# Expert results added up in DRAM by an accumulating scatter, four sums per token in place of six rows

## The chip, the cores and the metric
The kernel runs on 1 core of a Trainium2 chip. The metric is device time in microseconds (us) of one execution; of three runs of the kernel before the median was 1647.67 us (1644.37 to 1648.11). Everything is float32.

The engines of the core work side by side and wait for each other only at semaphores: TensorE (PE, its weight loads are PEld), VectorE (DVE), ScalarE (ACT), GpSimd (POOL) and SyncE (SP). SP issues most of the DMAs from its queue; POOL issues the indirect ones, whose target rows are given by a column of indices. All DMAs run on the same 16 DMA engines.

## The reference, cut to what matters
A block of 4096 tokens of 256 numbers goes through a mixture of experts (FFN), a local and a global attention, and the same FFN again:

```python
x = x + 0.5 * ffn(layernorm(x))
x = x + attention(layernorm(x))
x = x + 0.5 * ffn(layernorm(x))

def ffn(x):                              # 4096 tokens, 256 wide, 32 experts, 6 per token
    scores = sigmoid(x @ gate.T);  sfc = scores + bias
    # 4 of the 8 groups of experts by their best sfc, then the 6 best experts of these
    _, topk_idx = top_k(where(group_kept, sfc, 0), 6)
    tw = take(scores, topk_idx);  tw = tw / tw.sum() * 2.5
    routed = sum over the 6 chosen experts e of tw_e * ((silu(x @ g_e.T) * (x @ u_e.T)) @ dn_e.T)
    shared = (silu(x @ sg.T) * (x @ su.T)) @ sd.T
    return routed + shared
```

## The kernel before, in words
`x` stays in SBUF (`xres`, 32 tiles of 128 tokens). Each FFN has three stages, and each engine runs its own written-out program through them. The order on an engine is that of the code; there is no scheduler.

**Routing** (`*_route`; in the second FFN it is woven into the attention, `*_pass_b`) goes by 16 pairs of tiles. DVE normalizes a pair, PE transposes it and makes the logits, DVE finds the six experts and each token's place among the rows of each expert (`v_route_groups`, `v_route_six`, `v_route_ranks`, `v_route_weights`, `v_route_slots`). A row of 320 floats is built for each token: 256 of the normed token, 32 weights (`COL_W`) and 32 destinations (`COL_DEST`), the latter from a running count over the chosen experts (`nth`) and the token's number times six (`tok6`). POOL scatters each row six times, once per expert, into `dispatch_rows` in DRAM (line 522: 12 indirect DMAs per pair). SP stores the transposed token tiles to `normed_transposed` (line 409), and in the first FFN it also loads the experts' weights between these stores (`load_experts`, lines 398 to 403), a piece per pair.

**Experts** (`*_experts`) works through 224 blocks of 128 dispatched rows. SP loads a block into one of four buffers `blk` (line 437). PE transposes it (line 638), multiplies by gate and up (`wgu`), transposes the gated result (line 667), and multiplies by `wdn`. DVE takes the block's weight column and destination column out of the row (`pick`, line 1325, twice), multiplies (line 1337), adds to the destination an offset that pushes rows beyond the block's last one out of bounds (line 1345), and copies the result from PSUM into one of four buffers `yb` (line 1347). POOL scatters the 128 rows of `yb` into `answers` (line 535), where each token has six rows of its own; rows out of bounds are not written. DVE may overwrite a `yb` buffer once the scatter from it, four blocks earlier, has landed (`s.scat`).

**Combining** (`*_combine`) goes tile by tile. SP loads the tile's transposed tokens (line 449) and its six answer rows per token in two DMAs, of four rows and of two (line 457). DVE adds them in pairs: 0+2 and 1+3 (line 1405), 4+5 (line 1408). POOL adds the three results to `xres` (line 549). PE computes the shared expert (16 and 4 weight loads by the trace's count), and DVE adds it (line 1389). The answers have two buffers (`ans`), so a tile's load is issued when the sum of two tiles earlier is done (`s.red`).

## Time and profile before

| | |
|---|---|
| time, median of 3 runs | 1647.67 us |
| the profiled execution, first to last instruction | 1952.5 us |
| PE busy | 1406.0 us (72%) |
| DVE busy | 1173.1 us (60%) |
| POOL busy | 985.2 us (50%) |
| ACT busy | 643.7 us (33%) |
| moved by DMA | 283.75 MB, mean 145 GB/s |
| read from DRAM / written | 152.10 MB / 139.46 MB |

The profiled execution has only its span, 1952.5 us; what lies around it is not shown, and it is already 304.8 us longer than the median of the runs. A duration of one instruction is read from it as it stands; the length of a whole stage may be longer than in a run without the profiler.

By stages of the span: routing of the first FFN 0 to 345 us, its table of blocks to 367, experts to 779, combining to 886, the global attention to 940, local attention with the second routing to 1400, table to 1430, experts to 1840, combining to the end.

### The profile page before, as it was taken

The page shows a single profiled execution, that of the slowest core. Times are in us where ns is not written, and L with a number is a line of the kernel's source. Part 1 is how long each engine was busy: PE and PEld are TensorE (multiplying, and loading weights), DVE is VectorE, ACT ScalarE, POOL GpSimd, SP SyncE. Part 2 cuts the span into 40 slices and gives each one's busy share as a digit, 9 for nine tenths or more (in the row PEclk, how much of TensorE's full clock was granted, in tenths as well). Part 3 has the DMA queues.
Part 4 walks back from the last instruction along what each step waited for, and adds up shares of the span by engine and source line. Part 5 has one row for each costly group of instructions (what it writes and reads, how often), then busy time and mean ns, then how long its engine had stood idle before and what let it go on. Part 6 is the DMA issues. An engine that isn't in the chain of part 4 may idle for free.

```text
span 1952.5 us, 48288 instructions
## 1 busy us (share of the span) xinstructions
PE 1406.0 (72%) x8734; PEld 1125.2 (58%) x8735; DVE 1173.1 (60%) x5408; ACT 643.7 (33%) x2344; POOL 985.2 (50%) x1050
## 2 busy tenths in 40 slices
PE   2211121499999999886877676776369999999996
PEld 2111111377777778873655464554257777777795
DVE  5444444466666666794565564645656666666586
ACT  1000000244444444110643343434134444454310
POOL 3555555355555555780043424334545555555587
PEclk9999999999999999997987777878579999999998
DMA  8444444345545553880021212112244554555498
GB/s 280 161 165 154 150 153 148 101 152 163 164 152 158 160 163 105 297 294 0 7 76 67 84 59 80 71 66 92 95 133 152 163 165 148 159 160 160 133 318 305
DMA packets 165350, 283.75 MB, mean 145 GB/s; under 512 B 30118, under 2 KB 117691, under 8 KB 165312
## 3 DMA queue, kind: packets, MB, share of 16 engines
q1 hardware_dynamic: 121216, 165.78, 28.1%
q0 software_dynamic: 39936, 113.33, 15.9%
q10 hardware_dynamic: 4160, 4.19, 0.6%
q8 instruction: 16, 0.26, 0.1%
q14 instruction: 22, 0.18, 0.0%
HBM read 152.10 MB, written 139.46 MB: 149 GB/s over the span
## 4 chain that ended last, share of the span: by engine, by line
PE 39%; DVE 20%; issue 16%; SPq 6%; another core or an unknown queue 6%; DMA 5%; POOL 4%; ACT 2%; DVEq 1%; POOLq 0%; ACTq 0%
PE ps L566 32%; PE ps L638 4%; POOL xres L549 3%; SPq L432 3%; DMA ans<-answers 2%; SPq L437 2%; PE ps L667 2%; DVE prob L1519 1%; DMA blk<-dispatch_rows 1%; DVE newt L1119 1%; DVE newt L1118 1%; DVE yb L1405 1%; DVE rstd L1120 1%; DVE ohs L1223 1%
## 5 line engine op out<-in xcount | busy, mean ns | idle before, releaser
L535 POOL DMA_INDIRECT answers<-yb,didx x448 | 441.2, 985 | 399.1 <-issue 302.9
L522 POOL DMA_INDIRECT dispatch_rows<-blk,idx x384 | 376.2, 980 | 520.5 <-DVE idx L1225 409.2
L566 PE MATMUL ps<-wgu,xbt 128*128 x1792 | 471.4, 386 | 3.4 <-ACT xbt L967 1.2
L566 PEld LDWEIGHTS ps<-wgu,xbt 128*128 128x128 f32 x1792 | 308.6, 192 | 35.7 <-issue 10.7
L566 PE MATMUL ps<-wdn,hbt 128*128 x896 | 278.6, 393 | 25.5 <-DVE yb L1347 16.1
L1337 DVE SCALAR_TENSOR_TENSOR hb<-ps,wcol,sg 128x128 f32<-128x128 f32 x448 | 157.2, 351 | 229.1 <-ACT sg L973 153.7
L1325 DVE SCALAR_TENSOR_TENSOR picked<-iota_e,etab,blk 128x32 f32<-128x32 f32 x896 | 190.3, 250 | 47.2 <-DMA blk<-dispatch_rows 11.5
L973 ACT ACTIVATE sg<-ps 128x128 f32<-128x128 f32 x448 | 124.7, 278 | 250.5 <-PE ps L566 128.8
L566 PEld LDWEIGHTS ps<-wdn,hbt 128*128 128x128 f32 x896 | 156.4, 190 | 80.7 <-issue 63.1
L967 ACT COPY xbt<-ps 128x256 f32<-128x256 f32 x448 | 167.5, 374 | 106.3 <-PE ps L638 100.2
L1347 DVE COPY yb<-ps 128x256 f32<-128x256 f32 x448 | 187.3, 418 | 13.2 <-remote 6.7
L638 PE MATMUL ps<-ident,blk 128*128 128x128 f32 x896 | 176.3, 279 | 20.4 <-DMA blk<-dispatch_rows 19.2
L977 ACT COPY hbt<-ps 128x128 f32<-128x128 f32 x448 | 119.2, 266 | 146.5 <-PE ps L667 109.1
L573 PE MATMUL ps<-ident,yb 128*128 128x128 f32 x128 | 35.5, 371 | 169.0 <-issue 90.4
L638 PEld LDWEIGHTS ps<-ident,blk 128*128 128x128 f32 x896 | 110.5, 143 | 66.9 <-DMA blk<-dispatch_rows 35.5
L566 PEld LDWEIGHTS ps<-blk,wsgu 128*128 128x128 f32 x1024 | 126.9, 197 | 9.5 <-DMA blk<-normed_transposed 6.4
L566 PE MATMUL ps<-blk,wsgu 128*128 128x128 f32 x1024 | 129.0, 281 | 3.1 <-DMA blk<-normed_transposed 3.1
L667 PE MATMUL ps<-ident,hb 128*128 128x128 f32 x448 | 122.6, 274 | 0.0
L549 POOL TENSOR_TENSOR xres<-xres,yb 128x256 f32 (+1 forms) x128 | 108.2, 845 | 27.6 <-DVE yb L1405 16.0
L573 PEld LDWEIGHTS ps<-ident,yb 128*128 128x128 f32 x128 | 21.7, 212 | 172.8 <-issue 101.8
L934 ACT COPY xnt<-ps 128x256 f32<-128x256 f32 x64 | 23.9, 373 | 239.6 <-PE ps L573 161.2
L1507 DVE TENSOR_REDUCE smax<-ps 128x8 f32<-128x512 f32 x32 | 22.1, 690 | 132.8 <-remote 127.4
(180 smaller groups left out, 2139.6 us busy)
## 6 DMA issues: line engine op xcount, KB each, us to landing
blk<-dispatch_rows SPq DMA_DIRECT2D x448, 160.0 KB
ans<-answers SPq DMA_DIRECT2D x64, 512.0 KB, 4.4
ans<-answers SPq DMA_DIRECT2D x64, 256.0 KB, 4.2
normed_transposed<-xnt SPq DMA_DIRECT2D x64, 128.0 KB
wgu<-in_gate_up SPq DMA_DIRECT2D x32, 256.0 KB
blk<-normed_transposed SPq DMA_DIRECT2D x64, 128.0 KB, 3.5
answers<-yb,didx POOLq DMA_INDIRECT x448
dispatch_rows<-blk,idx POOLq DMA_INDIRECT x384
```

The costliest lines, as they stand in the source:

```text
L522: pool.indirect_dma_start(out=rows_dram, out_offset=bass.IndirectOffsetOnAxis(ap=idx[:, q, k:k + 1], axis=0), in_=rows[:, q, :], in_offset ...
L535: pool.indirect_dma_start(out=answers_dram, out_offset=bass.IndirectOffsetOnAxis(ap=didx[:, q:q + 1], axis=0), in_=yb[:, q, :], in_offset= ...
L549: pool.tensor_tensor(xtile(i), xtile(i), sums, ALU.add).then_inc(s.part, 1)
L566: return nc.tensor.matmul(out_, lhs, rhs, start=start, stop=stop)
L638: m = pe.transpose(ps[:, TX + q % 2, c * P:(c + 1) * P], blk[:, q, c * P:(c + 1) * P], ident[:])
L667: pe.transpose(ps[:, HT + 1 - j, 0:P], hb[:, 1 - j, :], ident[:]).then_inc(s.ht, 1)
L967: act.copy(xbt[:, j, :], ps[:, TX + j, 0:D]).then_inc(s.xt, 1)
L973: act.activation(sg[:, j, :], ps[:, GU + j, 0:I], ACT.Silu).then_inc(s.sg, 1)
L977: act.copy(hbt[:, 1 - j, :], ps[:, HT + 1 - j, 0:P]).then_inc(s.hts, 1)
L1325: v.scalar_tensor_tensor(out=picked[:, k, :], in0=iota_e[:], scalar=etab[:, bass.ds(n, 1)], in1=blk[:, q, col:col + E], op0=ALU.is_equal, ...
L1337: v.scalar_tensor_tensor(out=hb[:, j, :], in0=ps[:, GU + j, I:2 * I], scalar=wcol[:, q:q + 1], in1=sg[:, j, :], op0=ALU.mult, op1=ALU.mult ...
L1347: v.tensor_copy(yb[:, k, :], ps[:, DN + j, 0:D]).then_inc(s.y, 1)
```

## The change: what it does
1. The scatter of an expert's result adds to the row in DRAM (`compute_op=ALU.add`) in place of writing a row of its own. There are four tensors of sums (`answer_sums0` to `3`, 4096+128 rows of 1 KB each); block `n` adds into sum `n % 4`, whose buffer `yb[n % 4]` is also reused only when that scatter has landed, so no two scatters into one sum are under way together. Rows beyond a block's end are no longer left out: they go to row 4096 + partition, which nobody reads.
2. The sums are zeroed by SP during each routing (`zero_sums`): per pair of tiles four DMAs of 256 KB, and with the first pair four more of 128 KB for the last rows. POOL waits for all of them before the first scatter of an FFN.
3. A dispatched row has one destination (the token's number) in place of 32: 289 floats in place of 320. The running count `nth` goes from the routing, and in the experts stage the second `pick` and the addition of the offset become one instruction on 128x1 numbers.
4. Combining loads four rows per token, in four DMAs of 128 KB, adds them with one DVE instruction, and POOL adds two results to `xres` in place of three.

```diff
-ROW = D + 2 * E
+ROW = D + E + 1
-NOWHERE = 2 * T * TOPK
+NOWHERE = 2 * T
+NACC = 4
-        answers_dram = nc.dram_tensor("answers", [T * TOPK, D], F32).ap()
+        sums_dram = [nc.dram_tensor(f"answer_sums{k}", [T + P, D], F32).ap() for k in range(NACC)]
+        def zero_sums(sp, p):
+            for k in range(NACC):
+                sp.dma_start(sums_dram[k][bass.ds(p * (2 * P), 2 * P)].rearrange("(a p) d -> p a d", p=P),
+                             padt[:, 0:D].unsqueeze(1).to_broadcast([P, 2, D])).then_inc(zeroed, 16)
+                if isinstance(p, int):
+                    sp.dma_start(sums_dram[k][T:T + P], padt[:, 0:D]).then_inc(zeroed, 16)
             def load_answers(i, j):
-                for k, (a, b) in enumerate(PARTS):
-                    positive(sp, s.red, i * 2 - 3 + k)
-                    part = slice(a * D, b * D)
-                    sp.dma_start(ans[:, j, part], ans_v[bass.ds(i, 1)][:, :, part].rearrange("a p d -> (a p) d")
-                                 ).then_inc(s.ans[k][j], 16)
+                positive(sp, s.red, i - 1)
+                for k in range(NACC):
+                    sp.dma_start(ans[:, j, k * D:(k + 1) * D], sums_dram[k][bass.ds(i * P, P)]
+                                 ).then_inc(s.ans[j], 16)
         def pool_experts(pool, s):
-            with pool.Fori(0, NB // 4) as g:
-                for q in range(4):
-                    pool.wait_ge(s.y, g * 4 + (q + 1))
+            pool.wait_ge(zeroed, 16 * ZEROS * (s.n + 1))
+            pool.sem_inc(s.take, 1)
+            with pool.Fori(0, NB // 8) as g:
+                for r in range(8):
+                    q = r % 4
+                    pool.wait_ge(s.y, g * 8 + (r + 1))
                     pool.sem_inc(s.take, 1)
                     pool.indirect_dma_start(
-                        out=answers_dram, out_offset=bass.IndirectOffsetOnAxis(ap=didx[:, q:q + 1], axis=0),
-                        in_=yb[:, q, :], in_offset=None, bounds_check=T * TOPK - 1,
-                        oob_is_err=False).then_inc(s.scat[q], 16)
+                        out=sums_dram[q], out_offset=bass.IndirectOffsetOnAxis(ap=didx[:, r:r + 1], axis=0),
+                        in_=yb[:, q, :], in_offset=None, compute_op=ALU.add).then_inc(s.scat[q], 16)
         def v_route_weights
-            for t in range(2):
-                st.did(v.tensor_tensor_scan(nth[:, t, :], ones[:, 0:E], sel[:, t, :], 0.0, ALU.mult, ALU.add))
-            for t in range(2):
-                st.did(v.tensor_scalar(rows[:, 2 * k + t, COL_DEST:ROW], nth[:, t, :],
-                                       tok6[:, bass.ds(p * 2 + t, 1)], None, ALU.add))
+            st.did(v.tensor_copy(rows[:, two, COL_DEST], token_of[:, bass.ds(p * 2, 2)]))
         def v_experts, pick
-                for k, (col, out_) in enumerate(((COL_W, wcol), (COL_DEST, dcol))):
-                    v.scalar_tensor_tensor(
-                        out=picked[:, k, :], in0=iota_e[:], scalar=etab[:, bass.ds(n, 1)],
-                        in1=blk[:, q, col:col + E], op0=ALU.is_equal, op1=ALU.mult,
-                        accum_out=out_[:, q:q + 1]).then_inc(s.pick, 1)
+                v.scalar_tensor_tensor(
+                    out=picked[:], in0=iota_e[:], scalar=etab[:, bass.ds(n, 1)],
+                    in1=blk[:, q, COL_W:COL_W + E], op0=ALU.is_equal, op1=ALU.mult,
+                    accum_out=wcol[:, q:q + 1]).then_inc(s.pick, 1)
+                v.scalar_tensor_tensor(
+                    out=didx[:, r:r + 1], in0=skip[:, bass.ds(n, 1)], scalar=blk[:, q, COL_DEST:COL_DEST + 1],
+                    in1=dump[:], op0=ALU.add, op1=ALU.min).then_inc(s.pick, 1)
         def v_experts, step
-                    st.did(v.tensor_tensor(didx[:, k:k + 1], dcol[:, k:k + 1], skip[:, bass.ds(n - 2, 1)], ALU.add))
                     v.wait_ge(s.d, n - 1)
                     v.tensor_copy(yb[:, k, :], ps[:, DN + j, 0:D]).then_inc(s.y, 1)
-                    st.sync()
         def v_combine, body
                 v.tensor_tensor(two_sums[j], a[:, 0:2, :], a[:, 2:4, :], ALU.add).then_inc(s.red, 1)
-                v.wait_ge(s.ans[1][j], 16 + visits(i, j, 2, 16))
-                positive(v, s.part, i * 3 - 3)
-                v.tensor_tensor(third_sum[j], a[:, 4, :], a[:, 5, :], ALU.add).then_inc(s.red, 1)
         block.sync
                 load_experts(sp, p)
+                zero_sums(sp, p)
-            sp_route(sp, R[1])
+            sp.wait_ge(C[0].red, NT)
+            sp_route(sp, R[1], lambda p: zero_sums(sp, p))
```

DVE in the middle of the experts stage (`hb` is the gated result, `yb` the buffer that is scattered; `ans` in these rows is the memory that holds the table of offsets), before:

```order
L1337 SCALAR_TENSOR_TENSOR hb<-ps,wcol,sg 128x128 [waits ex_pick_0,ex_ht_0,ex_sg_0]
L1345 TENSOR_TENSOR didx<-dcol,ans 128x1
L1347 COPY yb<-ps 128x256 [waits ex_d_0]
L1325 SCALAR_TENSOR_TENSOR picked,wcol<-iota_e,etab,blk 128x32 [waits ex_pick_0,ex_h_0,ex_ld1_0,vector_step]
L1325 SCALAR_TENSOR_TENSOR picked,dcol<-iota_e,etab,blk 128x32
```

The same block of DVE's program after:

```order
L1342 SCALAR_TENSOR_TENSOR hb<-ps,wcol,sg 128x128 [waits ex_pick_0,ex_ht_0,ex_sg_0]
L1351 COPY yb<-ps 128x256 [waits ex_d_0]
L1326 SCALAR_TENSOR_TENSOR picked,wcol<-iota_e,etab,blk 128x32 [waits ex_h_0,ex_pick_0,ex_ld1_0]
L1331 SCALAR_TENSOR_TENSOR didx<-ans,blk,dump 128x1
```

The instruction on `didx` moved from ahead of the copy to behind the pick, and one of the two picks on 128x32 is gone.

SP's queue in the loop of combining, for one tile (`cb_gu`: the shared gate and up of an earlier tile is done; `cb_red`: the sum of two tiles earlier), before:

```order
L449 ISA [waits cb_gu_0]
L449 DMA blk<-normed_transposed 128x256
L49 ISA
L457 ISA [waits cb_red_0]
L457 DMA ans<-answers 128x1024
L49 REGISTER_ALU
L457 ISA [waits cb_red_0]
L457 DMA ans<-answers 128x512
```

and after:

```order
L458 ISA [waits cb_gu_0]
L458 DMA blk<-normed_transposed 128x256
L465 ISA [waits cb_red_0]
L465 DMA ans<-answer_sums 128x256 x4
```

The two loads of a tile's answers, each behind its own wait, became four loads behind one wait.

SP's queue in the loop of the first routing, for one pair, after (before, it ended with the loads of `wgu`):

```order
L420 DMA normed_transposed<-xnt 128x256
L400 ISA
L400 DMA dispatch_rows<-padt 128x289
L400 ISA
L400 DMA dispatch_rows<-padt 128x289
L401 ISA
L401 DMA wdn<-in_down 128x512
L405 REGISTER_ALU
L405 DMA wgu<-in_gate_up 128x512
L405 ISA
L405 DMA wgu<-in_gate_up 128x512
L409 ISA
L409 DMA answer_sums<-padt 128x2x256 x4
```

Four DMAs of 256 KB now stand between a pair's stores and the next pair's.

## Rows read from the trace of the kernel before

**Rows 1.** Windows by stage: busy us of each engine, granted clock, DMA share, GB/s.
```profile
0.00:345.00 345.00, 75.80 (x288) 59.36 (x289) 164.76 (x746) 26.21 (x66) 183.30 (x211) 1.00 0.50 172
367.00:779.00 412.00, 390.31 (x2053) 317.65 (x2054) 266.77 (x1570) 191.47 (x675) 219.81 (x224) 1.00 0.50 152
779.00:886.00 107.00, 87.92 (x605) 80.26 (x603) 91.75 (x208) 11.53 (x30) 82.56 (x97) 0.93 0.80 270
940.00:1400.00 460.00, 322.77 (x2825) 238.04 (x2823) 263.98 (x1026) 194.04 (x826) 169.73 (x173) 0.78 0.19 71
```

**Rows 2.** Windows, the same columns: ten us inside one pair of the second routing.
```profile
1175.50:1185.50 10.00, 3.56 (x16) 1.36 (x20) 0.31 (x2) 1.01 (x1) 6.17 (x7) 0.61 0.31 115
```

**Rows 3.** Timeline of PEld in the experts stage: start, us, engine, line, what.
```profile
601.19 0.73 PEld L566 LDWEIGHTS ps<-wgu,xbt 128*128 128x128 f32 x4
...
602.82 0.73 PEld L566 LDWEIGHTS ps<-wgu,xbt 128*128 128x128 f32 x4
```

**Rows 4.** POOL's scatters: one of a run in routing, and all of line 535.
```profile
206.00 0.97 POOL L522 DMA_INDIRECT dispatch_rows<-blk,idx  x1 [0.30 <-issue]
...
L535 POOL DMA_INDIRECT answers<-yb,didx x448: 982/985/1004, 379.4 to 1843.2; - x150
```

**Rows 5.** The page's DMA queues: packets, MB, share of 16 engines.
```profile
q1 hardware_dynamic: 121216, 165.78, 28.1%
q0 software_dynamic: 39936, 113.33, 15.9%
```

**Rows 6.** Timeline at the end of the first experts stage.
```profile
778.64 0.98 POOL L535 DMA_INDIRECT answers<-yb,didx  x1 [2.59 <-issue]
...
781.37 1.75 SPq L457 DMA_DIRECT2D ans<-answers  x4
```

**Rows 7.** Two DVE groups of the experts stages by line: min/median/max ns, waits.
```profile
L1345 DVE TENSOR_TENSOR didx<-dcol,ans x448: 142/150/202, 377.6 to 1838.3; 128x1 int32<-128x1 f32 x150
...
L1325 DVE SCALAR_TENSOR_TENSOR picked<-iota_e,etab,blk x896: 241/250/305, 370.3 to 1834.1; 128x32 f32<-128x32 f32 x180
...
  DVE hb L1337: 22.0, 28
```

**Rows 8.** Groups of the window 800 to 870 us, in the first combining.
```profile
L549 POOL TENSOR_TENSOR xres<-xres,yb 128x256 f32 x47 | 38.3, 816 | 4.4 <-POOL xres L549 4.4
L1405 DVE TENSOR_TENSOR yb<-ans 128x512 f32<-128x512 f32 x24 | 22.0, 917 | 0.0
...
L1408 DVE TENSOR_TENSOR red<-ans 128x256 f32<-128x256 f32 x12 | 11.4, 948 | 0.0
```

**Rows 9.** Timeline of one tile of the first combining.
```profile
831.03 1.97 PEld L566 LDWEIGHTS ps<-blk,wsgu 128*128 128x128 f32 x16
...
833.09 0.73 PEld L566 LDWEIGHTS ps<-wsd,hsh 128*128 128x128 f32 x4
```

**Rows 10.** The page's DMA issues: KB each, median us from issue to landing.
```profile
ans<-answers SPq DMA_DIRECT2D x64, 256.0 KB, 4.2
...
blk<-normed_transposed SPq DMA_DIRECT2D x64, 128.0 KB, 3.5
```

**Rows 11.** Timeline of DVE in one pair of the first routing.
```profile
228.66 0.21 DVE L1202 TENSOR_TENSOR cw<-sc,sel 128x64 f32<-128x64 f32 x1
228.80 0.39 DVE L1205 TENSOR_TENSOR_SCAN nth<-ones,sel 128x32 f32<-128x32 f32 x2
...
229.39 0.22 DVE L1210 TENSOR_REDUCE csum<-cw 128x2 f32<-128x64 f32 x1 [0.20 <-issue]
229.53 0.39 DVE L1212 TENSOR_SCALAR blk<-nth,tok 128x32 f32<-128x32 f32 x2
```

**Rows 12.** Timeline of DVE: first work behind a pair's last routing step (second routing).
```profile
1167.43 0.68 DVE L1507 TENSOR_REDUCE smax<-ps 128x8 f32<-128x512 f32 x1
```

**Rows 13.** The start: the window 0 to 30 us, and ACT's second pair.
```profile
0.00:30.00 30.00, 7.84 (x30) 6.01 (x31) 16.60 (x80) 3.93 (x9) 6.42 (x29) 1.00 0.90 286
...
32.63 0.37 ACT L934 COPY xnt<-ps 128x256 f32<-128x256 f32 x1 [10.68 <-DMA normed_transposed<-xnt]
```

More of the change, by code:

```diff
@@ L266, in build @@
         padded = sem("padded")
+        zeroed = sem("zeroed")
         consts = sem("consts")
@@ L317, in __init__ @@
                 s = lambda name: sem(f"{name}_{n}")
-                self.ans = [[s(f"cb_ans{part}_{j}") for j in range(2)] for part in range(2)]
+                self.ans = [s(f"cb_ans{j}") for j in range(2)]
                 self.xs = [s(f"cb_xs{q}") for q in range(4)]
@@ L1344, in step @@
                              16 * ((n - 2) // 4) if isinstance(n, int) else n * 4 - (8 + 4 * k))
-                    st.did(v.tensor_tensor(didx[:, k:k + 1], dcol[:, k:k + 1], skip[:, bass.ds(n - 2, 1)], ALU.add))
                     v.wait_ge(s.d, n - 1)
                     v.tensor_copy(yb[:, k, :], ps[:, DN + j, 0:D]).then_inc(s.y, 1)
-                    st.sync()
                 if m is None or n + 2 < NB:
-                    pick(n + 2, (q + 2) % 4)
+                    pick(n + 2, (r + 2) % 8)
             pick(0, 0)
             pick(1, 1)
-            for n in range(4):
-                step(n, n % 4, m=0)
-            one = 1
-            with v.Fori(1, NB // 4 - 1) as g:
-                for q in range(4):
-                    st.rebase(g * (4 * one) + (start + q - 2))
-                    step(g * 4 + q, q)
-            st.rebase(start + NB - 4 - 2)
-            for n in range(NB - 4, NB + 2):
-                step(n, n % 4, m=0)
+            for n in range(8):
+                step(n, n, m=0)
+            with v.Fori(1, NB // 8 - 1) as g:
+                for r in range(8):
+                    step(g * 8 + r, r)
+            for n in range(NB - 8, NB + 2):
+                step(n, n % 8, m=0)
         def v_combine(v, st, s, last):
```

43 lines of the change are left out of this document (20 added, 23 removed).

## The prediction, made before the changed kernel was run
> **What bounds the kernel now.** I read the windows by stage first, since the page's shares average over stages with different limits. The two experts stages last 412 us each and PE is busy for 390 of them [rows 1]; in a stretch without a disturbance a block of 128 rows follows the last after 1.63 us (601.19 to 602.82, and the two after it the same), in which the weight loads have no gap worth naming [rows 3]. So PE sets the pace there. Over the whole stage a block takes 412/224 = 1.84 us. Combining takes 107 us for 32 tiles; DVE is busy for 92, PE 88, POOL 83: three engines near their limit, none alone. In the routings nothing is: 345 us with DVE 165 and POOL 183 busy [rows 1].
>
> Then I asked why the profiled span (1952.5 us) is 304.8 us longer than the median of the runs. Within one pair of the second routing there are ten microseconds in which PE, DVE and ACT all nearly stop, while POOL goes on issuing scatters (DVE 0.31 us busy of 10) [rows 2]. If it returned in each of the 16 pairs it would make 160 us; the first routing has the like. I take these stalls for an effect of the recording and the timed kernel as shorter mainly in the routings. That is an inference. It matters twice: a gain that is read in a stall is worth nothing, and in a timed run the first routing is near POOL's pace: 12 scatters at 0.97 + 0.30 = 1.27 us make 15.3 us per pair [rows 4], 244 us for 16 pairs. My sum is in us of unstalled rows, so that it can be set against either: span 1952.5 or median 1647.7.
>
> **Part 1, the scatter into the sums.** The instruction is there 448 times as before, and its duration is 0.985 us now; the scatter without a bounds check, in routing, takes 0.97 [rows 4]. The trace has no accumulating DMA, so three costs are open.
> (a) POOL's own time. Hidden as long as duration plus 0.30 stays under PE's 1.63, that is up to 1.33 us. Lower bound 0.97, upper bound: twice the row, 1.97, which makes 2.27 us a block, +0.64 x 448 = +287 us. I take 0.98, the nearest row: the indices and rows that POOL handles are as many as before.
> (b) Time of the DMA engines. POOL's queue used 15.9% of the span for 832 scatters: 0.159 x 1952.5 / 832 = 0.37 us of all 16 engines per scatter. SP's queue used 0.281 x 1952.5 = 549 us for 121216 packets, 0.072 us per packet on one engine, so a block's load of 128 rows is 128/16 x 0.072 = 0.58 us [rows 5]. Together 0.95, under 1.63. An accumulating scatter reads its target as well. Bounds: 0.37 (the addition is free) and 4 x 0.37 = 1.5 (every row moved four times); I take twice, 0.75: it reads rows from two places in place of one, and of the two ends the plain scatter is the row at hand. 0.58 + 0.75 = 1.33 is still hidden. The point from which it isn't is 1.63 - 0.58 = 1.05 us, 2.8 times the plain scatter; at the upper bound a block takes 2.08, +0.45 x 448 = +200 us. That rows beyond a block's end are now written (448 x 128 = 57344 in place of 49152) is +17% and within this.
> (c) Landing. From the end of the last scatter's issue, 778.64 + 0.98 = 779.62, to SP's first load behind it, 781.37, are 1.75 us [rows 6]. A `yb` buffer is free for four blocks, 6.5 us, of which copy, wait and issue take some 2; landing may take 4.5 before DVE waits. I take 3.5 us. Hidden but for the end of each stage, where combining waits for the last: 2 x 1.75 = +3.5 us.
>
> The Trainium skill bears on (b): "Collectives: The Full Stack", section "The bandwidth ceiling", says that a reducing transfer is not slowed by the addition but by its two source reads, and moves data at about half a copy's rate. No row here shows it. By it the engines' time doubles, as I took it, and rival A needs more than that; the sum by the plain row alone would be the same, since both are hidden.
>
> **Part 2, zeros.** Per routing 4 x 4224 x 1 KB = 17.3 MB more. Combining moves 270 GB/s at a DMA share of 0.80, so 337 GB/s at full share, and the zeros are 51 us of all engines. The first routing has 0.50 x 345 = 172 us of DMA work [rows 1], 223 with them, against some 245 to 345 us of stage: room, but not much in a timed run. The second has 0.19 x 460 = 87, 138 with them: hidden. At the very start there is no room: the first 30 us run at a share of 0.90, and ACT already waits 10.68 us for the stores of the first pair, which stand in the same queue [rows 13]. The zeros of the first pair (1.57 MB, 5 us at 337 GB/s) now stand ahead of the second pair's stores, and 3 us more ahead of each of the next. Later pairs follow POOL's pace, so this is paid about once: +5 us. Bounds 0 (POOL's pace absorbs it) and +14 (5 + 3 x 3). The wait on `zeroed` costs nothing: all zeros are issued with the last pair's stores, and the table of blocks (some 22 us) lies between these and the first scatter.
>
> **Part 3, one destination per row.** In routing DVE loses two scans and two additions per pair. The scans: the sum `csum` starts at 229.39 behind `cw`, which ends at 228.87; without the scans between them it starts some 0.15 later than that, 0.37 earlier than now. The additions take 0.39 where one copy of 128x2 takes about 0.15 [rows 11]: together 0.6 us per pair. In the second routing this is on the path: DVE goes from the last routing step of a pair into the next tile's maximum without an idle time (its row names none) [rows 12], for which ACT and PE wait. 16 x 0.6 = 9.7; I take -8. In the first routing POOL's 15.3 us per pair bound a timed run, and I take 0 (it would be -9.6 if DVE set the pace). In the experts stage DVE loses 0.15 and one of two picks with its accumulator read, 0.25 + 0.08, and gains one instruction on 128x1, about 0.15: 0.3 us per block off an engine that is busy 267 of 412. PE bounds, so nearly nothing; but the gated product waited 22.0 us for picks, 28 times [rows 7], and so I take -3, between 0 and -22. Rows of 289 floats in place of 320 are 10% fewer bytes in a queue that isn't full: 0.
>
> The Trainium skill speaks against gaining from the narrower row: "DMA: Bandwidth & Descriptors", section "How a descriptor splits into AXI transactions", says that a read that doesn't start at a multiple of 256 B is fetched from the boundary below. 320 floats are 1280 B, five such pieces; 289 are 1156 B and nearly never start on one, so about as much is fetched. No row here shows it. Without the rule a block's load would take 0.52 us of the engines in place of 0.58 and a scatter could take 1.11 before it binds; with it the point stays at 1.05.
>
> **Part 4, combining.** 24 tiles in 70 us are 2.92 us a tile [rows 8]. Per tile DVE loses the instruction of line 1408 (0.95 us) and POOL one of three additions (at least 0.82). PE remains with 1.97 + 0.73 = 2.70 [rows 9]. But the loads now bind: a buffer is filled again only behind the sum of two tiles earlier. SP issues four loads, 0.44 us apart (1.75 for four [rows 6]), the last lands 3.5 us later (the row for 128 KB [rows 10]), and the sum takes 0.68 to 0.92: 1.32 + 3.5 + 0.8 = 5.6 us for two tiles, 2.80 a tile. So PE and the loads are within 0.1 of each other. Before, one load of 4.2 us and one sum made 5.1. I take 2.80: 64 x 0.12 = -8 us. Bounds: PE's 2.70, -14 us; and landing no faster than the 256 KB load, 4.2, with the sum at 0.92: 3.2 a tile, +19 us. The first sum of each combining waits for two more issues per tile, 3 x 0.44 = 1.3 us: +3.
>
> **Sum.** +3.5 (last scatters) + 5 (start) - 8 (second routing) - 3 (experts) - 8 + 3 (combining) = -7.5 us: span 1945, median 1647.7 - 7.5 = 1640.
>
> **Rivals.**
> A, the scatter becomes the bound (slower). Mechanism: a block's accumulating scatter takes more than 1.33 us of POOL or 1.05 us of the DMA engines, and PE waits through `yb` for `s.scat`. For it speaks that nothing in the trace shows the price, and that 448 blocks multiply it: 0.1 us of excess is 45 us. Against it the slack in (a) to (c). With POOL's 0.985 half as long again, 1.48 + 0.30 = 1.78 a block, +0.15 x 448 = +67, the time is 1707; three times the DMA time, 0.58 + 1.12 = 1.70, makes +31 and 1671.
> B, DVE's relief counts fully (faster). The waits for picks go (-22 more or less), the first routing is DVE's after all (-9.6), combining reaches PE's 2.70: 1640 - 19 - 9.6 - 6 = 1605, with the half of it 1622.
> C, the gains are eaten: SP's five DMAs and their landing keep combining at 2.92 a tile and the crowded start costs 14: 1640 + 8 + 9 = 1657, with one of the two 1648.
> That the change doesn't do what it says would need sums still read as six rows; SP's rows show four, so I give it nothing.
>
> **How the numbers follow.** Forecast 0.50 (its own range 1630 to 1650), A 0.24, B 0.12, C 0.14. A measurement of this kernel tells 0.3% (5 us) from no change; faster is below 1642.7. The forecast's half gives 0.30 faster, 0.14 same, 0.06 slower; B 0.12 faster; C 0.07 same and 0.07 slower; A 0.24 slower. Faster 0.42, same 0.21, slower 0.37. The range takes in C, half of B and A up to half as long again on POOL: 1615 to 1712; what lies beyond are the upper bounds of (a) and (b), 1840 and more, and B in full.
>
> **What would show it.** The line of the scatter still at 0.97 to 1.0 us and experts stages of 412 us or a little less: Part 1 right. Scatter above 1.33 us, or DVE's copy to `yb` waiting for DMAs: A. The DMA share in the experts windows from 0.50 to about 0.7 shows twice the engine time. Tiles of combining 2.8 us apart with DVE waiting for loads: Part 4. ACT's second wait for the stores grown from 10.68 by some 5 us: Part 2. `csum` 0.15 us behind `cw`, and the second routing shorter by 8 us: Part 3. The prediction is wrong if the experts stages differ by more than 10 us, or if the zeros slow the routings all along; and the profiled stalls may themselves grow with the DMA packets, which would lengthen the span and not the time.

## The result: 5.3% slower, and the profile after

| kernel | median of the runs, us | lowest to highest |
|---|---|---|
| before | 1646.02 | 1642.23 to 1648.11 |
| after | 1731.97 | 1731.80 to 1734.19 |

The ratio is 1.0533 (95% interval 1.0517 to 1.055): +86 us. 1640 had been forecast, with a range of 1615 to 1712, and 1731.97 lies above the range too.

The profiled execution of after has a span of 1732.4 us, no longer than its runs. That of before had 304.8 us more than its median, so stages can't be compared with it. The first experiment below records the unchanged kernel again, with a span of 1649.1 us; all comparisons by stage are made with that recording. It is of the slowest of that kernel's eight runs, 3.6 us over their median, so a difference of a stage is sure to some 3 us only. The stages follow from the starts of POOL's scatters and of the first instruction of the second FFN's routing; the second routing ends here where its last scatter starts:

| stage | before, us | after, us | difference | forecast |
|---|---|---|---|---|
| start to the first scatter of an expert | 288.0 | 293.9 | +5.9 | +5 |
| experts 1, first to last scatter | 363.5 | 415.9 | **+52.4** | -1.5 |
| combining 1 and global attention | 146.2 | 137.6 | -8.7 | -0.75 |
| local attention and second routing | 362.1 | 351.4 | -10.6 | -8 |
| table of blocks, to the first scatter | 15.1 | 13.8 | -1.3 | 0 |
| experts 2 | 363.9 | 414.2 | **+50.3** | -1.5 |
| combining 2 to the end | 110.3 | 105.6 | -4.7 | -0.75 |

(The forecasts of Part 3's -3 and of Part 4 with the last scatters, -8 + 3 + 3.5, are halved over the two stages of a kind.) The differences sum to +83.3, the difference of the spans. Two stages lose 103 us and the rest gains 19.

The windows by stage (those of experts and of the second routing reach to the end of the last scatter, 1 us further than the table; window, its length, then busy us of PE, PEld, DVE, ACT and POOL with their instructions, granted clock, DMA share, GB/s), first of the unchanged kernel's second recording, which answers to [rows 1]:

```profile
0.00:288.00 288.00, 87.51 (x336) 69.04 (x338) 175.91 (x810) 31.28 (x79) 192.67 (x219) 1.00 0.63 216
288.00:652.50 364.50, 363.62 (x2024) 317.37 (x2024) 262.16 (x1543) 186.13 (x663) 220.21 (x224) 1.00 0.56 168
...
797.70:1160.80 363.10, 276.60 (x2988) 219.83 (x2988) 286.26 (x1103) 202.73 (x864) 190.82 (x192) 0.89 0.27 98
```

and of after:

```profile
0.00:293.90 293.90, 86.76 (x332) 68.43 (x334) 168.16 (x753) 30.81 (x78) 191.71 (x220) 0.97 0.78 258
293.90:711.40 417.50, 401.72 (x2032) 302.47 (x2031) 242.47 (x1103) 186.37 (x664) 349.51 (x224) 1.00 0.92 148
...
847.40:1199.80 352.40, 267.45 (x2988) 212.40 (x2988) 277.74 (x1055) 203.02 (x864) 191.66 (x192) 0.92 0.41 142
```

In the experts stage before, PE is busy for all of it (363.62 of 364.50). From the first to the last of the 224 scatters are 363.5 us and 223 steps: a block takes 1.63 us. After, POOL's 224 scatters cost 349.51 us in place of 220.21, the DMA share is 0.92 in place of 0.56, and the GB/s fall. PE's busy time has grown with the stage, to 401.72 of 417.50: the same matmuls, stretched by waits that the profile counts into them. Read alone, that row still looks like a kernel bound by PE; the weight loads, which shrank from 317.37 to 302.47 while the stage grew, say that it isn't.

Rows of POOL's timeline in the middle of that stage (start, duration, what, idle time before it), which answer to [rows 4]:

```profile
402.13 1.56 POOL L546 DMA_INDIRECT answer_sums<-yb,didx  x1 [0.30 <-issue]
404.00 1.56 POOL L546 DMA_INDIRECT answer_sums<-yb,didx  x1 [0.31 <-issue]
405.87 1.56 POOL L546 DMA_INDIRECT answer_sums<-yb,didx  x1 [0.30 <-DVE yb L1351]
```

One scatter starts every 1.86 us: 1.56 of its own and the 0.30 that stood between scatters of a run in routing before. So there is no slack left on POOL, and 415.9/223 = 1.865 is the stage's own pace. The page's queues, to be held against [rows 5], and its groups of the scatter and of the copy to `yb`:

```profile
q0 software_dynamic: 82944, 115.59, 39.9%
q1 hardware_dynamic: 175616, 176.01, 34.5%
...
L546 POOL DMA_INDIRECT answer_sums<-yb,didx x448 | 697.3, 1556 | 162.8 <-issue 123.1
...
L1351 DVE COPY yb<-ps 128x256 f32<-128x256 f32 x448 | 189.7, 423 | 305.9 <-DMA answer_sums<-yb,didx 298.3
```

Two suspects stand here side by side. POOL issues the scatter for 1556 ns in place of 985. And DVE waits 298.3 us for scatters to land, while q0's share has grown to 39.9%. In the window 400 to 500 us the queues' shares are these:

```profile
q0 software_dynamic: 7696, 7.01, 64.5%
q1 hardware_dynamic: 7739, 7.95, 28.8%
issues: line engine op xcount, KB each, median us to landing
blk<-dispatch_rows SPq DMA_DIRECT2D x53, 144.5 KB
answer_sums<-yb,didx POOLq DMA_INDIRECT x54
```

64.5/54 = 1.19 us of all 16 engines per scatter and 28.8/53 = 0.54 per load, together 1.73 us a block: over PE's 1.63 as well, and under POOL's 1.86. Which of the two sets the pace is what most experiments ask. One row of this trace bears on it already, the first scatter of the stage:

```profile
293.88 1.61 POOL L546 DMA_INDIRECT answer_sums<-yb,didx  x1 [14.05 <-DVE yb L1351]
```

In the 12.8 us before it (281 to 293.8) not one packet of POOL's queue moves, so no earlier scatter can hold it up, and it takes 1.61 us all the same; the first of the second stage takes 1.60. The length is the instruction's own and not a wait behind a full queue.

### The profile page after: what moved, and what is told of

Same layout as the page of the kernel before. It is cut to its first block, busy times and chain, and to the rows that moved or that the text cites. A ratio compares the mean times of both kernels' runs of the same rounds, so it can differ in the third digit from the quotient of the medians.

```text
span 1732.4 us, 46430 instructions
## 1 busy us (share of the span) xinstructions
PE 1359.6 (78%) x8734; PEld 1061.8 (61%) x8735; DVE 1058.4 (61%) x4352; ACT 643.6 (37%) x2344; POOL 1174.1 (68%) x987
## 3 DMA queue, kind: packets, MB, share of 16 engines
q0 software_dynamic: 82944, 115.59, 39.9%
## 4 chain that ended last, share of the span: by engine, by line
issue 23%; DMA 22%; POOL 20%; PE 13%; DVE 12%; SPq 5%; ACT 1%; POOLq 1%; DVEq 1%; ACTq 0%
DMA answer_sums<-yb,didx 17%; PE ps L576 11%; POOL answer_sums L546 10%; POOL dispatch_rows L531 10%; DMA ans<-answer_sums 4%; SPq L465 3%; DVE yb L1351 2%; DVE prob L1517 1%; ACT ans L1054 1%; PE ps L881 1%; DVE yb L1406 1%; DMA dispatch_rows<-blk,idx 1%; DVE smax L1505 1%; DVE stats L1143 1%; PE ps L648 1%
## 5 line engine op out<-in xcount | busy, mean ns | idle before, releaser
L546 POOL DMA_INDIRECT answer_sums<-yb,didx x448 | 697.3, 1556 | 162.8 <-issue 123.1
L1351 DVE COPY yb<-ps 128x256 f32<-128x256 f32 x448 | 189.7, 423 | 305.9 <-DMA answer_sums<-yb,didx 298.3
L576 PEld LDWEIGHTS ps<-wgu,xbt 128*128 128x128 f32 x1792 | 306.6, 191 | 38.2 <-issue 12.8
L576 PE MATMUL ps<-wdn,hbt 128*128 x896 | 290.2, 406 | 15.0 <-DVE yb L1351 12.3
L576 PEld LDWEIGHTS ps<-wdn,hbt 128*128 128x128 f32 x896 | 145.0, 189 | 102.8 <-issue 94.8
L648 PE MATMUL ps<-ident,blk 128*128 128x128 f32 x896 | 172.8, 275 | 33.7 <-DMA blk<-dispatch_rows 33.7
L559 POOL TENSOR_TENSOR xres<-xres,yb 128x256 f32 (+1 forms) x128 | 93.5, 731 | 98.1 <-DVE yb L1406 86.5
L677 PE MATMUL ps<-ident,hb 128*128 128x128 f32 x448 | 127.7, 285 | 12.8 <-DVE hb L1342 12.7
L1326 DVE SCALAR_TENSOR_TENSOR picked<-iota_e,etab,blk 128x32 f32<-128x32 f32 x448 | 112.5, 251 | 31.4 <-DMA blk<-dispatch_rows 31.4
L677 PEld LDWEIGHTS ps<-ident,hb 128*128 128x128 f32 x448 | 62.8, 140 | 65.9 <-DVE hb L1342 56.7
L1406 DVE TENSOR_TENSOR yb<-ans 128x512 f32<-128x512 f32 x64 | 46.8, 731 | 82.2 <-DMA ans<-answer_sums 74.0
L1331 DVE SCALAR_TENSOR_TENSOR didx<-ans,blk,dump 128x1 int32<-128x1 f32 x448 | 96.5, 215 | 0.0
```

The lines of the kernel that those rows point to most:

```text
L546: pool.indirect_dma_start(out=sums_dram[q], out_offset=bass.IndirectOffsetOnAxis(ap=didx[:, r:r + 1], axis=0), in_=yb[:, q, :], in_offset= ...
L576: return nc.tensor.matmul(out_, lhs, rhs, start=start, stop=stop)
L648: m = pe.transpose(ps[:, TX + q % 2, c * P:(c + 1) * P], blk[:, q, c * P:(c + 1) * P], ident[:])
L677: pe.transpose(ps[:, HT + 1 - j, 0:P], hb[:, 1 - j, :], ident[:]).then_inc(s.ht, 1)
L1326: v.scalar_tensor_tensor(out=picked[:], in0=iota_e[:], scalar=etab[:, bass.ds(n, 1)], in1=blk[:, q, COL_W:COL_W + E], op0=ALU.is_equal, op ...
L1331: v.scalar_tensor_tensor(out=didx[:, r:r + 1], in0=skip[:, bass.ds(n, 1)], scalar=blk[:, q, COL_DEST:COL_DEST + 1], in1=dump[:], op0=ALU.a ...
```

## The experiments

Ratios are against the kernel before, run beside them on the same chip.

### The unchanged kernel, recorded again


> The kernel before once more, for a second profile of it. In its first profile the span was 1952.5 us against timed runs of 1646, with stretches in which every engine nearly stood. If these stretches belong to that one recording, this profile's span lies within 5 us of the timed runs, an experts stage lasts 224 x 1.63 to 1.70 = 365 to 380 us and a pair of the second routing about 21 us. If they belong to the kernel under any recording, the span is again above 1900.

Measured: 1647.47 us, ratio 0.9998 (0.9983 to 1.0013), span 1649.1. The experts stages last 363.5 and 363.9 us, just under the 365 to 380 expected. The 304.8 us of stalls in the first recording are not the kernel's. No recording of after or of the kernels below has any, though POOL's queue moves twice the packets in after (82944 against 39936). What set them off in that one stays open.

### The scatter writes in place of adding
```diff
-    in_=yb[:, q, :], in_offset=None, compute_op=ALU.add).then_inc(s.scat[q], 16)
+    in_=yb[:, q, :], in_offset=None).then_inc(s.scat[q], 16)
```
All else is as in after; the sums then hold only each row's last write.

> The changed kernel with a plain write in the scatter in place of the addition (the sums are then wrong: the last block's row stays). Theory issue: the addition makes POOL's instruction 1.56 us in place of 0.97, and 1.56 + 0.30 = 1.86 per block is over PE's 1.63; theory landing: it makes the DMA work of a scatter about 1.2 us of all engines and its landing 4.9, and DVE waits for the buffer. Both expect POOL's instruction at 0.97, experts stages of 365 to 380 us, and a time of 1732 - 2 x (416 - 372) = 1644, less if the other parts gain what I forecast (1636 to 1646). Rival rest: the zeros, the dump rows and the four loads cost the 86 us; then the time stays above 1700.

Measured: **1630.31 us, ratio 0.9899 (0.9882 to 0.9915)**. First the window of its first experts stage, then POOL's timeline and POOL's queue in the window 400 to 500 us (62 scatters):

```profile
293.70:658.70 365.00, 364.12 (x2028) 318.72 (x2027) 218.14 (x1103) 186.80 (x664) 217.50 (x224) 1.00 0.55 169
```
```profile
399.39 0.97 POOL L546 DMA_INDIRECT answer_sums<-yb,didx  x1 [0.57 <-issue]
401.09 0.97 POOL L546 DMA_INDIRECT answer_sums<-yb,didx  x1 [0.73 <-issue]
```
```profile
q0 software_dynamic: 2928, 8.00, 20.2%
```

Scatter 0.97, idle time of 0.57 and 0.73 before these two, PE bound again; the time is 6 us under the range expected (1636 to 1646), since the stages are shorter than the 372 us it was reckoned with. One keyword costs 1731.97 - 1630.31 = 102 us, all of it in the experts stages (364.0 and 364.0 us). Against the kernel before, run beside this one (1647.41), zeros, routing, combining and the row format together gain 17 us. Excess by POOL's cadence: (1.86 - 1.63) x 448 = 103.

### Eight buffers and eight sums
```diff
-        sums_dram = [... for k in range(NACC)]
+        sums_dram = [... for k in range(8)]
...
-                    k = (q + 2) % 4
+                    k = (r + 6) % 8
...
-                    v.tensor_copy(yb[:, k, :], ps[:, DN + j, 0:D]).then_inc(s.y, 1)
+                    v.tensor_copy(result(k), ps[:, DN + j, 0:D]).then_inc(s.y, 1)
```
`result(k)` is `yb` for four buffers and unused memory of the stage for the others; eight sums are zeroed and scattered into, combining still reads four of them.

> The changed kernel with eight result buffers and eight sums in the experts stage, so that a buffer is free for eight blocks and two scatters into one sum still never overlap; twice the zeros are written, and combining still reads only four of the eight sums (half of the results are left out). Theory issue: DVE's waits for landed scatters (298 us now) go, yet a block still takes 1.86 us and the experts stages stay at 416; the time is 1732 plus what 17 MB more zeros per routing cost (0 to 30). Theory landing by latency: the experts stages shrink to 365 to 380 us and the time by 80. If it is the DMA engines' work, not the latency, the stages stay at about 224 x 1.74 = 390 or more.

Measured: 1740.08 us, ratio 1.0567 (1.0545 to 1.059); scatters 1.56 us, 1.86 apart. DVE's waits in the window 400 to 500 us (engine, line, waited for: us, times, longest; `ans` names the memory of the four further buffers):

```profile
DVE yb L1354 <- DMA answer_sums<-yb,didx: 19.0, 24, 1.6
DVE ans L1354 <- DMA answer_sums<-ans,didx: 17.9, 21, 1.6
```

I had expected these waits to go. They stayed, 36.9 us against 35.8 in after, and twice the room moved nothing. So the 298.3 us are a symptom: behind a pace maker slower than PE the ring of buffers fills up, and the producer then waits for its oldest buffer, with eight as with four. The timelines of DVE's copies and POOL's scatters, matched in order, show where a result stands: from the end of its copy to the start of its scatter are 0.8 us with the plain write, 2.7 in after and 10.0 here (medians of the first stage). The results wait for POOL. Landing is not the bound. Of the 5.4 us by which its span (1737.8) exceeds after's, 4.0 lie ahead of the first scatter, where twice the zeros are written.

### Sums of half the width
```diff
-            in_=yb[:, q, :], in_offset=None, compute_op=ALU.add).then_inc(s.scat[q], 16)
+            in_=yb[:, q, 0:D // 2], in_offset=None, compute_op=ALU.add).then_inc(s.scat[q], 16)
```
The four sums have 128 columns; the second half of a result isn't added, and combining reads the first half twice.

> The changed kernel with sums of 128 numbers per row: the scatter adds only the first half of each result, and combining reads that half twice (half of the results are left out). The DMA work of a scatter falls from 1.2 to 0.6 to 0.9 us of all engines and it lands sooner; the number of rows and indices that POOL handles stays. Theory issue: POOL's instruction stays at 1.56 and the experts stages at 416. Theory landing or DMA work: the stages shrink towards 365 to 380, and POOL shows idle time between its scatters.

Measured: 1737.34 us, ratio 1.0552 (1.0535 to 1.057), first experts stage 416.1 us. Queue shares in the window 400 to 500 us, and POOL's timeline:

```profile
q0 software_dynamic: 7774, 3.54, 33.8%
q1 hardware_dynamic: 7774, 7.99, 31.7%
```
```profile
398.05 1.56 POOL L547 DMA_INDIRECT answer_sums<-yb,didx  x1 [0.30 <-issue]
399.92 1.56 POOL L547 DMA_INDIRECT answer_sums<-yb,didx  x1 [0.30 <-issue]
```

Half the bytes take half the engines' time (33.8/54 = 0.63 us per scatter in place of 1.19), the total falls to 1.21 us a block, well under PE's 1.63, and not a microsecond comes back. They also land sooner: DVE's waiting copies start 3.5 us behind the start of the scatter that frees their buffer, in after 4.4 (medians). **The DMA engines are not the bound, nor is landing, and the 1.56 us are not back-pressure of bytes.** The number of packets is unchanged, though, so this run alone doesn't exclude a price per packet. Why the time is 5 us over after's isn't explained; combining, which reads each half row twice, may be a part of it.

### One more instruction on POOL per scatter, and its control
```diff
                         in_=yb[:, q, :], in_offset=None, compute_op=ALU.add).then_inc(s.scat[q], 16)
+                    pool.wait_ge(s.fill, g * 8 + (r + 1))
+                    pool.sem_inc(ppassed, 1)
+                    pool.memset(idle[:], 0.0).then_inc(s.fill, 1)
```
(`fill` is a new semaphore, raised once ahead of the loop, so that a memset waits for the one before and not for the scatter; `idle` is 128x1.)

> The changed kernel with one more small POOL instruction behind each of the 448 scatters (a memset of 128x1, 0.1 to 0.13 us, with 0.05 to 0.2 us around it). Theory issue (POOL's 1.56 + 0.30 us per block are the bound): every block is longer by what the filler takes, 0.15 to 0.3 us, so 67 to 135 us on 1732. Rival (the landing of the scatters or the DMA engines' work is the bound, 1.74 of 1.86 us by their shares): POOL's filler fills a wait, and the time moves by less than 20 us.

The same three lines in the kernel before (with `g * 4 + (q + 1)`):

> The same filler in the kernel before, as the control. There POOL needs 1.28 us per block of PE's 1.62: with 0.15 to 0.3 more it is at 1.43 to 1.58, still below, and theory issue expects no change (within 5 us of 1647). If the filler costs the same here as in the changed kernel, it slows something else than POOL's queue, and the reading of the other run falls.

Measured: with the filler after takes 1740.69 us (ratio 1.0566, 1.0546 to 1.0585), only 8.7 more; before takes 1646.46 (1.0000, 0.9987 to 1.0012). POOL's timelines, of after with the filler and then of before with it:

```profile
400.32 0.71 POOL L554 MEMSET idle<- 128x1 f32 x1
401.23 1.57 POOL L549 DMA_INDIRECT answer_sums<-yb,didx  x1 [0.19 <-POOL idle L554]
402.21 0.70 POOL L554 MEMSET idle<- 128x1 f32 x1
403.10 1.57 POOL L549 DMA_INDIRECT answer_sums<-yb,didx  x1 [0.19 <-POOL idle L554]
```
```profile
399.19 0.13 POOL L544 MEMSET idle<- 128x1 f32 x1
399.75 0.98 POOL L538 DMA_INDIRECT answers<-yb,didx  x1 [0.43 <-POOL idle L544]
```

The control is as expected. The test is a miss: by its number alone (8.7 us, under the 20 of the expectation) it is what the rival of landing or DMA work had forecast. The rows show why it can't decide. I had taken the filler to stand behind the scatter with its full time. Its row starts 0.98 us after the scatter's start, as in the control, and lasts 0.70 us in place of 0.13; it ends 0.11 us behind the scatter, and the next scatter starts 0.30 us behind the last one, as without a filler. So the filler fits into the 0.30 us that stand between two scatters anyway, and doesn't price POOL. Whether the memset worked beside the scatter or only stood there until the scatter's end, the rows don't say.

### Half the rows
```diff
-   out=sums_dram[q], out_offset=bass.IndirectOffsetOnAxis(ap=didx[:, r:r + 1], axis=0),
-   in_=yb[:, q, :], in_offset=None, compute_op=ALU.add).then_inc(s.scat[q], 16)
+   out=sums_dram[q], out_offset=bass.IndirectOffsetOnAxis(ap=didx[0:P // 2, r:r + 1], axis=0),
+   in_=yb[0:P // 2, q, :], in_offset=None, compute_op=ALU.add).then_inc(s.scat[q], 16)
```
Rows 64 to 127 of every block are not added.

> The changed kernel whose scatter adds only the first 64 rows of each block (the other 64 results are left out). It asks what sets POOL's 1.56 us. If it goes with the rows, the instruction falls to about half plus a fixed part, 0.8 to 1.1 us, PE is the bound again, and the time is 1630 as with the plain write. If it is a fixed cost of the addition, the instruction stays near 1.56 and the time near 1732.

Measured: 1666.23 us, ratio 1.0113 (1.0094 to 1.0132). POOL's timeline:

```profile
400.75 1.40 POOL L546 DMA_INDIRECT answer_sums<-yb,didx  x1 [0.30 <-issue]
402.46 1.40 POOL L546 DMA_INDIRECT answer_sums<-yb,didx  x1 [0.30 <-issue]
```

The queues in the window 400 to 500 us (60 scatters):

```profile
q0 software_dynamic: 4720, 3.87, 37.9%
q1 hardware_dynamic: 8423, 8.65, 32.7%
```

Neither expectation was met: 64 rows fewer take off 0.16 us, 2.4 ns a row, and by a straight line through the two some 1.25 us would remain with no row at all (an estimate). The cadence of 1.71 us predicts (1.71 - 1.63) x 448 = +36 us over the plain write; measured are +35.9. POOL's 1.86 and 1.71 thus each give the loss, where the DMA work was 1.73 and is (37.9 + 32.7)/60 = 1.18, under PE's pace. The number of packets doesn't price the instruction either: 63 fewer per scatter (4720/60 = 79 in place of 142) take off 0.16 us, so the 95 that separate an adding scatter from a plain one (47) would account for 0.24 of the 0.58 us.

### The addition in every other block
```diff
-                        in_=yb[:, q, :], in_offset=None, compute_op=ALU.add).then_inc(s.scat[q], 16)
+                        in_=yb[:, q, :], in_offset=None,
+                        **({} if q % 2 else dict(compute_op=ALU.add))).then_inc(s.scat[q], 16)
```
Sums 1 and 3 are written, not added to.

> The changed kernel with the addition in every other block and a plain write in the rest (the sums are then wrong). POOL's mean per block is (1.86 + 1.27) / 2 = 1.57 us, just below PE's 1.62. Theory issue expects a time of 1630 to 1640: the loss is a threshold, not a price per addition. If each addition costs the engines its own share, half of the 102 us stays and the time is about 1681.

Measured: **1625.98 us, ratio 0.9864 (0.9848 to 0.988)**, experts stage 362.8 us.

```profile
398.99 1.58 POOL L546 DMA_INDIRECT answer_sums<-yb,didx  x1 [0.30 <-issue]
400.87 0.98 POOL L546 DMA_INDIRECT answer_sums<-yb,didx  x1 [0.30 <-issue]
402.34 1.57 POOL L546 DMA_INDIRECT answer_sums<-yb,didx  x1 [0.50 <-issue]
```

Two blocks cost POOL 1.88 + 1.28 = 3.16 us, 1.58 each, under 1.63, and idle time is back (0.50). So 224 additions in two stages cost nothing, where 448 cost 102 us: a threshold, not a price per addition. The time is 4 us under the range expected (from 1630) and under the plain write's; why isn't explained.

### The first pair's zeros behind the routing
```diff
-                zero_sums(sp, p)
+                if not isinstance(p, int):
+                    zero_sums(sp, p)
             sp_route(sp, R[0], more)
+            zero_sums(sp, 0)
```


> The changed kernel with the zeros of the first pair (1.57 MB, eight DMAs) written by SP behind the whole first routing in place of ahead of the second pair's stores. If the 5.9 us by which the first scatter of the experts now starts later come from these zeros in the crowded start, 3 to 6 us come back and the time is 1726 to 1729. If they come from the zeros of all pairs, the first scatter stays at 294 us and the time at 1732.

Measured: 1731.42 us, ratio 1.051 (1.0495 to 1.0524), against after's 1.0533 (1.0517 to 1.055) no difference that can be told, where 1726 to 1729 had been expected. ACT's wait for the second pair's stores in after and in this kernel, answering to the row of ACT in [rows 13] (there 10.68; it belongs to the third pair, not to the second as is said there):

```profile
40.84 0.37 ACT L944 COPY xnt<-ps 128x256 f32<-128x256 f32 x1 [17.90 <-DMA normed_transposed<-xnt]
```
```profile
34.81 0.37 ACT L944 COPY xnt<-ps 128x256 f32<-128x256 f32 x1 [12.48 <-DMA normed_transposed<-xnt]
```

The first scatter starts at 288.8 in place of 293.9: the 5 us at the start are these zeros, through the stores that stand behind them. In after, SP issues the eight DMAs of zeros from 28.18 to 35.34 us, and only then the second pair's stores. But the gain was lost again further on: the second routing took 354.6 us in place of 351.4, and the two combining stages 1.5 us more. For the same 2988 matmuls PE was busy 272.5 us at a mean granted clock of 0.91, after's 267.45 at 0.92. Why the clock differed is open, and so is whether the late zeros had a part in it.

### Before, with one scan and one addition per pair
```diff
-            for t in range(2):
-                st.did(v.tensor_tensor_scan(nth[:, t, :], ones[:, 0:E], sel[:, t, :], 0.0, ALU.mult, ALU.add))
+            st.did(v.tensor_tensor_scan(nth[:].rearrange("p t e -> p (t e)"), ones[:, 0:2 * E],
+                                        sel[:, 0:2, :].rearrange("p t e -> p (t e)"), 0.0, ALU.mult, ALU.add))
...
-            for t in range(2):
-                st.did(v.tensor_scalar(rows[:, 2 * k + t, COL_DEST:ROW], nth[:, t, :],
-                                       tok6[:, bass.ds(p * 2 + t, 1)], None, ALU.add))
+            st.did(v.tensor_tensor(rows[:, two, COL_DEST:ROW], nth[:],
+                                   tok6[:, bass.ds(p * 2, 2)].unsqueeze(2).to_broadcast([P, 2, E]), ALU.add))
```
The count runs on through the second tile, and `tok6` starts six lower per token there.

> The kernel before, results unchanged, with the running count of a pair in one scan over 64 numbers in place of two over 32 (each token has exactly six chosen experts, so the second tile's count starts at six, which the table of token numbers takes off), and one addition in place of two. DVE saves about 0.3 us per pair. The change gained 10.6 us in the second routing by dropping all of this (0.6 us per pair); if DVE's order is what bounds a pair there, half of it comes with this: 3 to 6 us, a time of 1641 to 1644. If the gain came from the lighter traffic of the narrower rows or from the lost wait, nothing moves.

Measured: **1643.62 us against 1645.64, ratio 0.9983 (0.9974 to 0.9993)**. The window of the second routing:

```profile
794.30:1152.20 357.90, 273.35 (x2988) 218.04 (x2988) 282.49 (x1071) 202.96 (x864) 190.45 (x192) 0.90 0.27 99
```

DVE's busy time falls by 3.8 us against 286.26, the stage by 4.2 to 357.8. A part of these 4.2 us may be chance: the recording is of this kernel's fastest run, the one that it is compared with of the slowest of its own, and in the recording of the filler in the kernel before, whose routing is unchanged, the stage took 360.8. The medians differ by 2.0 us, with 3 to 6 expected. It is the fastest kernel here that computes everything, by less than 0.2%.

## Why the prediction was wrong, point by point

**The step that failed: Part 1 (a).** "I take 0.98, the nearest row: the indices and rows that POOL handles are as many as before." The point from which it binds (1.33 us) was right, the bounds (0.97 to 1.97) held the truth, 1.56, and PE's pace was 1.63, as taken. The step that failed is the term "duration of the scatter": 0.98 us taken, 1.56 measured, so that 0.23 us a block were not hidden. It was chosen by counting POOL's inputs, and these did not change. What the instruction turns out did: q0's packets are 7696/54 = 142 per scatter in the window 400 to 500 us, where the plain write shows 2928/62 = 47 there. But by the run with half the rows that number accounts for 0.24 of the 0.58 us at most; where POOL spends the rest of them stays open. The nearest row was the row of another operation. With 1.56 in the sum the forecast had been -7.5 + 0.23 x 448 = +96 us, 1743. That is rival A, at the size of 1.48 us given as its example (1707); it was given 0.24, and with the point from which it binds, 1.33, in the lower half of the bounds of an unknown price, the chance should have been nearer to a half. The range ended at 1712 because it let POOL's row grow by half; it grew by 58%.

The Trainium skill has the reading that was missing. "Perfetto Trace Analysis", section "DMA Instruction — SWDGE (GPSIMD)", says that the profiled end of a DMA issued by GpSimd is the end of its descriptor generation, not of the data's movement. The runs agree: half the bytes leave the row at 1.56 us, fewer rows shorten it, and the data land at 4.89 us (below), well behind its end. Of the stage's first scatter, whose row ends 1.61 us after its start, no packet moves for 2.9 us. So the row's 1.56 us are work on POOL ahead of the transfer, and POOL pays for the addition. The page gives no price for it, and that the added time is spent on descriptors is not shown here.

**Part 1 (b), DMA engines: direction right, size low.** Taken 0.75 us, measured 1.19; with the load of 0.54 (taken 0.58) 1.73 a block, over PE's 1.63, and a DMA share of 0.92 in the stage where about 0.7 had been named as the sign. It stayed hidden only behind POOL. If POOL's price went, by this sum the DMA engines would bind next and leave (1.73 - 1.63) x 448 = some 45 us; that is an estimate and wasn't tried. The Trainium skill, "Collectives: The Full Stack" (section "The bandwidth ceiling") would have it at half a copy's rate, thus twice 0.33 (plain write: 20.2/62); here it is 3.6 times. The measurement decides; the page took its rule from large collectives, and for this scatter of rows of 1 KB it falls short.

**Part 1 (c), landing: hidden as forecast, size roughly right.** The chain of waits has it from the scatter's start:

```profile
400.27 4.89 DMA answer_sums<-yb,didx
```

Less the 1.56 us of issue that is 3.3 us, where 3.5 were taken; by DVE's waiting copies it lies between 3.7 and 5.3 us from the scatter's start, 4.4 in the median. At the end of the first stage, from the last scatter's start at 709.82 to SP's first load at 713.64, are 3.8 us, as at the end of the second; in the unchanged kernel's second recording they are 3.1 and 2.2. That is +2.3 for both, forecast +3.5.

**Part 2, zeros: right.** +5.9 us at the start against +5, by the mechanism named; the wait on `zeroed` cost nothing, and the second routing took the zeros at a DMA share of 0.41 without a loss that shows (352.5 us with twice the zeros, 351.4 with these).

**Part 3: the routing right, the experts stage wrong by little.** DVE's timeline in one pair of the second routing after, to be read against [rows 11]:

```profile
1000.36 0.22 DVE L1212 TENSOR_TENSOR cw<-sc,sel 128x64 f32<-128x64 f32 x1
1000.78 0.22 DVE L1216 TENSOR_REDUCE csum<-cw 128x2 f32<-128x64 f32 x1 [0.20 <-DVE cw L1212]
1000.91 0.16 DVE L1217 COPY blk<-token_of 128x2 f32 x1
```

`csum` starts 0.20 us behind `cw` (0.15 forecast), and the copy takes 0.16. DVE's busy time in that stage falls by 286.26 - 277.74 = 8.5 us, the stage by 10.6 (forecast 8). The last experiment, with about half the relief, got 4.2 by its recording and 2.0 by its medians. The two points agree in direction with DVE as the pace maker there. They don't isolate it: the granted clock rose too, 0.89 to 0.90 and 0.92, and PE's busy time fell by 3.3 and 9.2. A relief in the experts stage is worth nothing: with the plain write they take 364.0 us, before 363.5 and 363.9, so -3 was too much. The narrower rows, which were to give nothing, gave next to nothing: over the first stage a block's load took 0.59 us of the engines before and 0.57 with the plain write, 4% less for 10% fewer bytes.

**Part 4, combining: direction right, size too small, and the loads not shown to be what binds.** DVE and SP's queue in the second combining, against [rows 8 to 10]:

```profile
1665.18 0.69 DVE L1406 TENSOR_TENSOR yb<-ans 128x512 f32<-128x512 f32 x1 [1.47 <-DMA ans<-answer_sums]
...
1667.70 0.70 DVE L1406 TENSOR_TENSOR yb<-ans 128x512 f32<-128x512 f32 x1 [1.18 <-DMA ans<-answer_sums]
...
1670.38 0.69 DVE L1406 TENSOR_TENSOR yb<-ans 128x512 f32<-128x512 f32 x1 [1.31 <-POOL xres L559]
```
```profile
1640.55 1.76 SPq L465 DMA_DIRECT2D ans<-answer_sums  x4
```
```profile
ans<-answer_sums SPq DMA_DIRECT2D x256, 128.0 KB, 2.5
```

DVE does wait for the loads, as forecast. Their median is 2.5 us; a tile's last load, which the sum is made with, takes 3.0 to 3.2 in the chain of waits, where I took the 3.5 of another load of 128 KB. With 3.1 and the sum's 0.69 the prediction's own sum gives (1.32 + 3.1 + 0.69)/2 = 2.6 us a tile, under PE's 2.70. In the six tiles from 1662.35 to 1678.73, 2.73 us each, PE is busy for 16.05 of 16.38 us and its weight loads for 14.68. A busy PE counts waits in, so these rows don't tell which of the two binds; the loads alone they don't show. Over all 32 tiles, from the first such sum to the last, a tile takes 2.71 us in the first combining and 2.91 in the second; in the unchanged kernel it takes 2.97 and 3.09, and the prediction had 2.92 and 2.80. Both combining stages together gave 13.4 us, forecast 1.5 with the last scatters.

**The stalls in the first recording: right,** and needed: the pace of 1.63 us per block read from an unstalled row [rows 3] is what the runs have, the 1.84 of the stage's mean isn't. By 1.84 the scatter would have seemed to have 0.2 us more room than it had.

## What to carry to other kernels

An instruction with one more option is another instruction: its price can't be read from a row without the option, and where the threshold lies inside the bounds, the far side is owed its share of the chance. Better still, measure that one instruction first. Count the slack of every engine in a loop at its pace in unstalled rows: here 0.35 us of slack per block stood against 0.58 us added, 448 times. And when a producer waits for its own buffers to come free, look for the engine with no idle time but the constant gap; here POOL had none, and twice the buffers gained nothing. To tell an instruction's own length from a wait behind a full queue, look at the first one of a stage, with nothing ahead of it.

## What the runs showed of the hardware that was not expected

- A scatter of 128 rows that adds takes POOL 1.56 us against 0.97; 64 rows 1.40; rows of 512 B as much as rows of 1 KB. The first of a stage, with the queue empty, takes 1.61. The next scatter starts 0.30 us behind the last one at the earliest, and a memset on POOL between them, 0.13 us elsewhere, leaves that gap at 0.30.
- Engine time of an adding scatter of 128 KB is 1.19 us of all 16 engines against 0.33 plain; of 64 KB 0.63, whether by 128 half rows (33.8/54) or by 64 whole ones (37.9/60). So it goes by bytes, and POOL's time doesn't.
- One recording held 18% of stalls (304.8 us over the median) that neither the runs nor the eleven later recordings have.
